# Moving two batches' roots and gates from ScalarE to GpSimd, and late routing steps to later tiles

## The reference

```python
xa = x @ Wm_attn.T                       # batch-normalised over all tokens, then split in q, k, v
att = softmax(causal(q @ k.T / sqrt(C)))
x = layernorm(x + (att @ v) @ W_proj.T @ Wm_proj.T)
probs = softmax(ln(x) @ router_w.T + router_b)
topw, topi = top_k(probs, 2)             # gates are topw / sum(topw)
out = sum over e of gate_e * (gelu(ln_e(x) @ W1_e.T + B1_e) @ W2_e.T + B2_e)
x = layernorm(x + out)
```

## Time and profile before

| | |
|---|---|
| Time, median of 3 runs | 430.28 us (429.62 to 431.0) |
| The profiled execution's own time | 429.71 us |
| Its span, first to last instruction | 428.0 us |
| Busy: PE, ACT, POOL, DVE | 94%, 76%, 75%, 67% |
| Mean granted clock of PE | 0.988 of full |
| Attention stage, hand-over, tiles | to about 137 us, 137 to 147 us, to 416 us |

### The profile page before, as it was taken

One profiled execution on the slowest core, in us unless ns is written; L12 is line 12 of the kernel. 1 busy time (PEld: TensorE's weight loads), 2 busy tenths in 40 slices (PEclk: granted clock), 3 DMA queues, 4 the chain that ended last, 5 costly groups with the idle time before them and its releaser, 6 DMA issues.

```text
span 428.0 us, 14581 instructions
## 1 busy us (share of the span) xinstructions
PE 403.6 (94%) x3454; PEld 386.2 (90%) x3458; DVE 284.7 (67%) x1676; ACT 324.5 (76%) x830; POOL 321.0 (75%) x605
## 2 busy tenths in 40 slices
PE   7988799999998999999999999999999999999980
PEld 6966787998887999999999999999999999999980
DVE  2446687999999777655556555446676666666662
ACT  1226688999888788777888887888888888888851
POOL 7000276888888888888888788748878888788885
PEclk9999999999999999999999999999999999999995
DMA  9999511111113432454544455642333334333211
GB/s 226 318 402 385 132 41 34 40 48 48 42 47 103 130 93 84 127 148 118 147 130 121 114 146 148 187 121 79 106 101 107 105 109 113 102 90 105 66 32 37
DMA packets 45490, 51.69 MB, mean 121 GB/s; under 512 B 6610, under 2 KB 37074, under 8 KB 45410
## 3 DMA queue, kind: packets, MB, share of 16 engines
q1 hardware_dynamic: 37312, 31.46, 27.4%
q0 software_dynamic: 7728, 18.51, 12.7%
q10 hardware_dynamic: 370, 0.80, 0.6%
HBM read 28.23 MB, written 21.72 MB: 117 GB/s over the span
## 4 chain that ended last, share of the span: by engine, by line
PE 53%; DVE 18%; issue 9%; POOL 9%; SPq 4%; DMA 4%; ACT 2%; POOLq 0%; DVEq 0%; ACTq 0%
PE bank L869 19%; PE bank L884 19%; POOL r_z L601 5%; POOL out L607 4%; PE bank L684 3%; DVE x_all L1284 3%; PE bank L859 2%; DVE st L1296 2%; PE bank L675 2%; DVE lg L1227 2%; DVE ix L1312 2%; PE bank L733 1%; DVE masked L1203 1%; DMA x_all<-x 1%; SPq L433 1%
## 5 line engine op out<-in xcount | busy, mean ns | idle before, releaser
L884 PE MATMUL bank<-w2T,xT 128*128 x1136 | 150.3, 275 | 0.7 <-DVE yt L1464 0.7
L869 PE MATMUL bank<-xT 128*128 128x128 f32 x1136 | 150.7, 276 | 0.0
L884 PEld LDWEIGHTS bank<-w2T,xT 128*128 128x128 f32 x1136 | 138.2, 192 | 0.9 <-issue 0.9
L869 PEld LDWEIGHTS bank<-xT 128*128 128x128 f32 x1136 | 138.0, 192 | 0.0
L921 ACT ACTIVATE xT<-w1T,zero_col 128x512 f32 x139 | 100.4, 722 | 40.7 <-issue 35.1
L1464 DVE TENSOR_TENSOR yt<-bank,b_bc 128x128 f32<-128x128 f32 x142 | 41.5, 292 | 89.0 <-PE bank L884 82.0
L607 POOL DMA_INDIRECT out<-xT,xg x71 | 75.9, 1069 | 16.9 <-issue 16.5
L594 POOL DMA_INDIRECT queue<-xT,xg x71 | 72.2, 1017 | 18.2 <-POOL idle L592 14.1
L1058 ACT ACTIVATE xT<-bank 128x512 f32<-128x512 f32 x142 | 82.1, 578 | 2.4 <-PE bank L869 2.4
L573 POOL DMA_INDIRECT queue<-x_all x64 | 62.2, 971 | 12.6 <-issue 7.9
L921 ACT ACTIVATE xT<-bank,one_col 128x128 f32<-128x128 f32 x142 | 52.1, 367 | 8.8 <-PE bank L859 3.4
(11 more groups left out here) (233 smaller groups left out, 729.2 us busy)
## 6 DMA issues: line engine op xcount, KB each, us to landing
xg<-queue SPq DMA_DIRECT2D x71, 129.5 KB, 2.1
xg<-queue SPq DMA_DIRECT2D x71, 67.5 KB, 2.2
x_all<-x SPq DMA_DIRECT2D x16, 256.0 KB, 6.1
xT<-x_t SPq DMA_DIRECT2D x8, 512.0 KB, 10.4
w1r<-w_t SPq DMA_DIRECT2D x8, 256.0 KB, 6.4
w2T<-w_t SPq DMA_DIRECT2D x8, 256.0 KB, 11.4
queue<-xT,xg POOLq DMA_INDIRECT x71, 2.9
out<-xT,xg POOLq DMA_INDIRECT x71, 2.4
```

The source lines that it names most:

```text
L869: last = mm(bank[2 + s][:, h * P:(h + 1) * P], w1c[:, (q - 1) % WR, h * P:(h + 1) * P], xgT[:, s, :], start=True, stop=True)
L884: last = mm(bank[4 + s][:, 0:P], hs[:, s, h, :], w2T[:, bass.ds(e, 1), h, :].rearrange("p a d -> p (a d)"), start=(h == 0), stop=(h == HC ...
```

## The change

It leaves what is computed the same and moves these steps.

- The roots of batches 30 and 31 go from ACT to POOL (`late_roots`), ahead of the scatters of batches 26 and 27. There they are three instructions each on 4 columns: multiply, add, power.
- LATE_GE goes from 2 to 4: the gates of batches 28 and 29 go from ACT to POOL as well.
- ACT loads gelu's table ahead of its last attention copy, and fetches W1 for tile 3 behind gelu of tile 0 instead of ahead of it.
- DVE routes batches 30 and 31 at tiles 4 and 6 and places them at tiles 7 and 9; PE ranks them at tiles 6 and 8; the count of the last batch goes from tile 7 to 11, and the making of the second table (`LIST_AT`, `TAKE_AT`) moves 4 tiles back.
- The eight dummy matmuls ahead of tile 2 go. Four small memsets join POOL's set-up.

```diff
-        LIST_AT, LIST_STEPS, TAKE_AT = 8, 12, 22
-
-        PE_STEP_AT_TILE = {2: NB + 2, 4: NB + 3}
-        DVE_STEP_AT_TILE = {1: NB + 2, 3: NB + 3}
+        LIST_AT, LIST_STEPS, TAKE_AT = 12, 12, 26
+
+        LATE_ROOTS = 2
+        ROOTS_BEFORE = {NB - 6: NB - 2, NB - 5: NB - 1}
+        RANK_AT_TILE = {6: NB - 2, 8: NB - 1}
+        ROUTE_AT_TILE = {4: NB - 2, 6: NB - 1}
+        PLACE_AT_TILE = {7: NB - 2, 9: NB - 1}
+        COUNT_AT = 11
 
         COUNT0 = NB0 + 3
 
-        LATE_GE = 2
+        LATE_GE = 4
...
+            pg.did(pool.memset(late_scale[:, :, 0:1], 1.0 + EPS_FFN))
+            pg.did(pool.memset(late_scale[:, :, 1:2], 1.0))
+            pg.did(pool.memset(late_eps[:, :, 0:1], EPS_POST * EPS_FFN))
+            pg.did(pool.memset(late_eps[:, :, 1:2], EPS_POST))
...
+            def late_roots(b):
+                pool.wait_ge(s_mv6, b + 1)
+                var = x_all[:, of_batch(b), ROOT:ROOT + 1].to_broadcast([P, TPB, 2])
+                pg.did(pool.tensor_tensor(late_ve[:], var, late_scale[:], ALU.mult))
+                pg.settle()
+                pg.did(pool.tensor_tensor(late_ve[:], late_ve[:], late_eps[:], ALU.add))
+                pg.settle()
+                pool.tensor_tensor(x_all[:, of_batch(b), ROOT:ROOT0 + 1], late_ve[:],
+                                   neg_half[:].rearrange("p (t n) -> p t n", t=TPB), ALU.pow).then_inc(s_rl, 1)
+
             BETWEEN = 3
             for b in range(NB):
+                if b in ROOTS_BEFORE:
+                    late_roots(ROOTS_BEFORE[b])
                 scatter(b)
...
-                if known in PE_STEP_AT_TILE:
-                    step = PE_STEP_AT_TILE[known]
-                    attend_step(step, step % U, 0, step)
+                if known in RANK_AT_TILE:
+                    rank(RANK_AT_TILE[known])
...
-                if known == 7:
+                if known == COUNT_AT:
...
             pe.wait_ge(s_tab, 1)
-            keep_warm(8)
             pe.wait_ge(s_w2, 16 * E)
...
             def last_steps():
                 copy_p(NB - 1)
                 copy_turned(0, 0)
-                roots(NB - 2)
-                gate(NB - 4)
                 copy_turned(1, 1)
-                roots(NB - 1)
-                gate(NB - 3)
                 act.wait_ge(s_tab, 1)
...
-                if 1 <= k < NTILE - AHEAD:
+                if 1 < k < NTILE - AHEAD:
                     fetch_w1(k + AHEAD, q + AHEAD)
...
+                if k == 1:
+                    fetch_w1(k + AHEAD, q + AHEAD)
+
+            act.preload_act_table_set("gelu_and_others")
             last_steps()
-            act.preload_act_table_set("gelu_and_others")
...
             def route(b):
 
-                v.wait_ge(s_rr, b + 1)
+                if b < NB - LATE_ROOTS:
+                    v.wait_ge(s_rr, b + 1)
+                else:
+                    v.wait_ge(s_rl, b - (NB - LATE_ROOTS) + 1)
...
                 ffn_step(k)
-                if k in DVE_STEP_AT_TILE:
-                    step = DVE_STEP_AT_TILE[k]
-                    attend_step(step, step % U, 0, step)
+                if k in PLACE_AT_TILE:
+                    place(PLACE_AT_TILE[k])
+                if k in ROUTE_AT_TILE:
+                    route(ROUTE_AT_TILE[k])
```

More of the change, by code:

```diff
@@ L360, in build @@
         ve_z, r_z = sb("ve_z", [P, 4]), sb("r_z", [P, 4])
-        neg_half = sb("neg_half", [P, 3])
+        neg_half = sb("neg_half", [P, 4])
+        late_ve, late_scale, late_eps = [sb(n, [P, TPB, 2]) for n in ("late_ve", "late_scale", "late_eps")]
+        s_rl = sem("s_rl")
         eps_0, eps_1 = sb("eps_0", [P, 1]), sb("eps_1", [P, 1])
@@ L545, in _ @@
             pool.wait_ge(s_var, 1)
-            pool.tensor_tensor(rstd[:], bn[:, MSQ, :], neg_half[:], ALU.pow).then_inc(s_rstd, 1)
+            pool.tensor_tensor(rstd[:], bn[:, MSQ, :], neg_half[:, 0:3], ALU.pow).then_inc(s_rstd, 1)
             def second_pads():
@@ L1066, in root @@
                 act.activation(ln_z[:, at], ve_z[:, at], ACT.Ln, bias=zero_col[:]).then_inc(s_ln, 1)
-                act.wait_ge(s_ln, NB + n + 1)
+                act.wait_ge(s_ln, NB - LATE_ROOTS + n + 1)
                 act.activation(r_z[:, at], ln_z[:, at], ACT.Exp, scale=-0.5).then_inc(s_ra, 1)
@@ L1269, in attend_step @@
                 has = {d: 0 <= k - d < NB for d in (0, 1, 2, 3, 4)}
+                has[3] = has[3] and k - 3 < NB - LATE_ROOTS
                 has[3] = has[3] and k - 3 > EARLY[-1]
```

## The result

| | before | after |
|---|---|---|
| time, median (lowest to highest) | 430.43 us (429.24 to 431.0) | 435.79 us (434.95 to 437.5) |
| profiled execution / its span | 429.71 / 428.0 us | 434.95 / 433.2 us |

The runs of before are those timed beside the changed kernel. The ratio is 1.0122, with a 95% interval of 1.0095 to 1.0148, which is 5.3 us of 430.43 (the medians lie 5.36 apart).

The account below looks back on a forecast made before the run. PE sets the tile stage's pace except at tile 29, which hangs on POOL's `send_on(4)`. POOL's 1.5 + 4.0 + 2.3 = 7.8 us on 429.71, with 0.57 for the median, gave 438.1 us; range 437.0 to 441.0.

Parts of the forecast that it names:

- POOL's extra work: On POOL ahead of `send_on(4)`: a wait, two `late_roots` and two gates add 1.5 + 4.0 + 2.3 = 7.8 us.
- The wait: On POOL ahead of scatter 26: the first `late_roots` waits 1.5 us (1.3 to 1.7) for batch 30's variances.
- the 0.4 us of restart: On POOL behind each `late_roots`: the memset and first DMA begin later, 0.4 us of the 2.0 charged.
- A fixed 197.87 - 167.13 = 30.74 us: From the start of POOL's `send_on(4)` to tile 29's start on PE: always 30.74 us.
- the link: Chain from `send_on(4)` through SP's eight load and pad pairs, last pad and load 29 to tile 29: 30.74 us.
- POOL's bounds: Limits on the sum of POOL's added wait and work: 7.0 to 8.6 us.
- PE's own progress up to it has no part in it: At tile 29: its start follows POOL's `send_on(4)` alone, whatever PE gains earlier.
- The front: Hand-over from attention to tiles 2 and 3: PE gains some 1.4 us, none of which reaches tile 29.
- rival 2: At tile 29: POOL's delay plus a fallen clock costing 1.5 us; 439.6 us, up to 442; chance 0.38.
- Tile 18: PE waits 4 us or more there for its late load, inside the 7.8 us; a clock fall costs nothing.
- Later steps that might bind instead have room: After POOL's new work: batch 31 is placed about 158 us, and POOL wants it after 165.

Follow-up runs that it names:

- g1: Kernel before with its eight pad writes issued earlier on SP (three behind load 16, three behind 17, one each behind 20 and 22): ratio 1.0006.
- h1: Changed kernel with seven dummy matmuls filling PE's two waits at the hand-over: ratio 1.013.
- h4: Changed kernel repeated in the fourth set: ratio 1.0134, 5.9 us more than the kernel before.
- g2: Changed kernel without POOL's late roots and the gates of batches 28 and 29, with g1's earlier pads and second table six tiles earlier: ratio 1.0005.
- h2: g2 with seven dummy matmuls filling PE's two waits at the hand-over: ratio 0.9998.
- f2: Changed kernel repeated in the second set: ratio 1.0101.
- g3: Changed kernel with g1's earlier pads and the second table six tiles earlier: ratio 1.0039.
- g4: g3 with the late roots one batch later, ahead of scatters 27 and 28: ratio 1.0031.
- e4: Changed kernel with its pads earlier (five behind load 17, one each behind 19, 21 and 23): 449.77 us, ratio 1.0076.
- e2: Changed kernel without POOL's new work (late roots and gates of batches 28 and 29 left out): 448.95 us, ratio 1.0066.
- i1: h2 with pads at other places (three behind load 17, one each behind 20, 22, 24, 25 and 26): 452.63 us, ratio 1.0086.
- e1: Kernel before with POOL's new work alone, written to tiles that nobody reads: 451.77 us, ratio 1.0129.
- f1: Kernel before repeated in the second set: ratio 1.0013.
- e3: Changed kernel with its late roots one batch later, ahead of scatters 27 and 28: 447.4 us, ratio 1.0034.
- f4: Kernel before with six idle powers on POOL ahead of scatter 26 and six ahead of scatter 28: ratio 1.0079.
- h3: g4 with seven dummy matmuls filling PE's two waits at the hand-over: ratio 1.0037.

## Why the prediction was off, step by step

- **POOL's extra work: 7.8 us, measured 7.4.** `send_on(4)` is 7.06 us later, and the attention stage of that execution ended 0.36 us earlier (first tile transpose at 137.72 against 138.08), so POOL's delay is 7.4. The wait was 1.56 us (forecast 1.5) and the power of four columns 1.05 (1.03). I charged 2.0 us for a `late_roots`; the first took 1.63, for the 0.4 us of restart behind it hardly showed: the memset follows at once, and the DMA waits 0.18 us, as it always does.
- **"A fixed 197.87 - 167.13 = 30.74 us": this step failed.** It was 28.73. The send landed in 2.47 and not 3.63 us, the last pad in 2.31 and not 3.64, together 2.49 less. Of that 0.6 was lost again, since load 21 then stood for the send of tile 5 (1.89 us behind load 20, before 1.30). I took two landings of one execution for constants. They were the longest part of the link (7.3 of 30.74 us) that no instruction explains, and should have been bounds: in the trace of the kernel before, the sends land in 2.6 to 4.3 us, with a median of 2.9. That the change itself brings the quick landings is what six traces suggest; by what means is not shown. The stated range could not have caught it: it was made from POOL's bounds and a fallen clock (by the prediction's own terms 437.3 to 442), with nothing for the landings.
- **"PE's own progress up to it has no part in it": too strong.** The idle piece of 0.40 us was the whole distance between PE and the link. g1 shows that the kernel before gains nothing when the link is cut.
- **The front, 1.4 us and worth nothing: right, with more causes than one.** It was 1.45 us in the first profile. The link takes it, as forecast (h1 against h4). Where the link is cut, the clock at the hand-over took it in g2, and in h2 the wait at tile 18, which my edit made.
- **The clock (rival 2, 0.38): it falls, but elsewhere.** No trace shows a fall at tile 29. So the 1.5 us of that rival, and the upper part of the range, had no counterpart. Falls came at the hand-over, with the wait of 1.08 us that the change makes longer, and at tile 18, where I had said that one costs nothing; for h1 that holds, and for h2, where PE is the bound, it cost 1.5 us. The Trainium skill (TensorE: Matmul & The Clock Gate, Part 1) has gaps in the feed bring the half clock back. The traces agree with it in direction, but behind the same wait of 1.1 us the clock fell in five traces (f2, g2, g3, g4, h4) and not in two (the first profile, e4).
- **Tile 18: 4 us forecast, 2.29 measured.** The send of tile 2 was issued 0.6 us earlier than I had it (170.81) and landed in 2.5 us and not 3.6, and DVE had the load 1.9 us behind its issue and not 2.4.
- **"Later steps that might bind instead have room": true of the changed kernel, and too narrow.** The second table, ready at 197.8 us and 2.6 us ahead of load 29, was not looked at; it bound in e2 and in e4. And the late placing of batch 30 has room only because POOL is late (e2, g2, h2 and i1).

With POOL at 7.4, 0.36 for the earlier attention stage and a link shorter by 2.0, tile 29 is 5.05 us later; 0.19 us came behind it, and the profiled times differ by 5.24.

**What is shown:** POOL's new work with its wait is enough to cause a loss of this size (e1); some two thirds of it, or more, run over the pads and the second table (g3); and the front gain does not reach the end in any version. **What stays open:** what holds back one or two of the sixteen shares of the last pad in before, f1 and e3 and not in the traces with a quick pad. Counted from `send_on(4)`, the DMA issues of f1 and f2 come in the same order and within 1 us of each other up to the last pad, so the order in the queues does not explain it. Open too: why the clock falls behind the same wait in some executions only; how the loss divides where the attention stage takes long, for there some of it seems to come behind tile 29 (from tile 29 to 70 it is 83.6 us in e1 and e4, whose POOL is 10 us late, and 80.5 to 80.9 in e2 and e3); and whether the front gain would reach the end with clock, POOL and SP all out of its way. No run had that: in e2, g2, h2 and i1 POOL waited for batch 30, and i1 was run where the attention stage took long.

## What to carry to other kernels

Work taken from the engine with a wait (ACT) and given to the engine whose queue frees the buffers (POOL) costs time as soon as the latter's path and that of the bound engine meet; look first at how much lies between them (0.4 us here, and more in the second set), since that is all that there is to win or to give. In a sum over a chain, take durations of instructions as fixed and landings as ranges, from several landings of the same kind in the trace. When a long chain is cut, list what each of its ends also waits for: here the second table was ready only 1.8 us before the last pad had landed, and the moved pads ran into a wait for their own counts. And when a part of a change is run alone, read the waits of every engine again: what the other part had hidden, here POOL's wait for batch 30, comes to light and is not what was to be measured.

## What the runs showed of the hardware

- A power on POOL takes 0.57, 0.75, 0.89 and 1.05 us for 1, 2, 3 and 4 columns of 128 rows, a multiply of 4 columns 0.20 us.
- The granted clock fell to 0.50 (1.2 GHz) with waits of PE of 1.1 us (g2, h4), 2.3 us (h1, h2) and 3.9 us (e4, i1), and in e1 and f4 with none above 0.6 us, for 3.4 to 6.8 us, and behind the same wait of 1.1 us it fell in some traces and not in others. With dummies in that wait (of which 0.2 us were left) it did not fall at the hand-over in h1, h2 and h3.
- A pad of 67.5 KB lands when the slowest of its 16 shares has: 1.6 to 2.3 us from its issue where all shares had ended by 1.53 us, 3.1 to 3.6 us where one or two had not. The sends of the first pass landed in 2.6 to 4.3 us (median 2.9) in the kernel before.
- SP's own instructions pace the pairs: a load and a pad take 2.4 us (from load 21, at 179.29, to load 28, at 196.16, it is 16.87 us for seven pairs, and up to 18.3 us in other traces), with the transfers themselves hidden.
- The same kernel on the same chip took 446.87 us in one set and 430.35 in another, and a kernel's first tile transpose came at 145.3 to 147.7 us in the one and at 137.5 to 137.8 in the other. From tile 29 to tile 70 it was 77.8 to 78.2 us in the sets at 430 us and 77.9 to 83.6 in the others; from tile 70 to the end 152.2 to 152.9 us in every trace.
